# A graph network's second edge scatter on GpSimd: issued in portions beside the first layer's attention, router and experts, instead of all beside the experts

## What is computed

```python
edge_index = jnp.stack([src, dst])
xn = _layernorm(x, axis=-1)
x = x + _L0_gnn_ref(xn, edge_index, ...) + _L0_mix_ref(xn[None], L0_mix_Wq, L0_mix_Wkv, L0_mix_Wproj, L0_mix_bproj)[0]
x = x + _L0_ffn_ref(_layernorm(x, axis=-1)[None], ...)[0]      # router and 6 experts, top 2
xn = _layernorm(x, axis=-1)
x = x + _L1_gnn_ref(xn, src, dst, ...) + _L1_mix_ref(xn[None], ...)[0]
...
```

## Time and profile before

| | |
|---|---|
| median of three executions | 7550.93 us (7548.48 to 7556.42) |
| profiled execution, its own time | 7552.14 us |
| its span in the profile | 7550.2 us |
| granted TensorE clock, mean | 0.838 of full speed |
| busy: TensorE matmuls | 5770.7 us, 76% |
| busy: VectorE / ScalarE / GpSimd | 4088.7 / 2739.3 / 3202.7 us |

### The profile page before, as it was taken

The page is one execution under the profiler, slowest core; times in us unless marked ns, Lnnn a source line. Parts: engine busy times, 40 slices in busy tenths (PEclk is TensorE's granted clock), DMA queues, the critical chain, the costliest instruction groups (busy, mean ns, idle before and its releaser), DMA issues. The chain is left out here.

```text
span 7550.2 us, 91454 instructions
## 1 busy us (share of the span) xinstructions
PE 5770.7 (76%) x22573; PEld 3591.7 (48%) x22664; DVE 4088.7 (54%) x9995; ACT 2739.3 (36%) x7575; POOL 3202.7 (42%) x3209
## 2 busy tenths in 40 slices
PE   5564688888985788876976787998788858998386
PEld 3332355554542565642545553554455535565253
DVE  7876577733113899966245334213577775556401
ACT  2524477721220444410114432113166615555010
POOL 1776576404772666610017750000177715553101
PEclk9999788888997778778988887898778766987597
DMA  2534222100001655510013330000144423333222
GB/s 87 165 86 155 50 50 47 31 12 28 2 2 53 172 158 157 159 32 13 0 60 105 105 75 23 0 0 14 47 117 115 112 58 105 98 98 69 76 99 74
DMA packets 268803, 549.15 MB, mean 73 GB/s; under 512 B 86992, under 2 KB 136588, under 8 KB 263692
## 3 DMA queue, kind: packets, MB, share of 16 engines
q0 software_dynamic: 134496, 314.63, 16.6%
q1 hardware_dynamic: 133932, 230.20, 9.5%
HBM read 495.56 MB, written 49.00 MB: 72 GB/s over the span
## 5 line engine op out<-in xcount | busy, mean ns | idle before, releaser
L1252 POOL DMA_INDIRECT L_edges_rows<-scratch_L_kv,L_edges_index x416 | 496.8, 1194 | 379.7 <-PE L_edges_ps_sum L1501 213.0
L1252 POOL DMA_INDIRECT L3a_edges_rows<-scratch_L3a,L3a_edges_index x416 | 462.5, 1112 | 409.5 <-DMA L3a_edges_last<-order_dst_last 257.1
L1252 POOL DMA_INDIRECT L3b_edges_rows<-scratch_L3b,L3b_edges_index x416 | 398.6, 958 | 400.8 <-PE L3b_edges_ps_sum L1501 236.3
L1702 POOL TENSOR_TENSOR L_norm_fold<-L_norm_square 128x400 f32<-128x400 f32 x64 | 66.6, 1040 | 1168.3 <-ACT L_norm_square L1711 1168.3
L482 POOL DMA_INDIRECT scratch_by_dst<-dst_record,dst_dest x400 | 439.7, 1099 | 271.1 <-DVE dst_dest L334 149.5
L1252 POOL DMA_INDIRECT L_edges_rows<-scratch_L,L_edges_index x416 | 424.4, 1020 | 257.3 <-issue 117.8
L632 POOL DMA_INDIRECT L_edges_rows<-scratch_L,L_edges_index x416 | 396.8, 954 | 274.5 <-SPq L616 148.0
L2324 DVE TENSOR_TENSOR L_experts_gated_h<-L_experts_hidden,L_experts_ps_g 128x800 f32<-128x800 f32 x112 | 110.6, 988 | 665.0 <-PE L_experts_ps_g L2277 665.0
L482 POOL DMA_INDIRECT scratch_by_src<-src_record,src_dest x400 | 383.1, 958 | 124.0 <-issue 121.7
L2315 ACT ACTIVATE L_experts_hidden<-L_experts_ps_h,L_eb_sb 128x400 f32<-128x400 f32 x320 | 190.2, 594 | 646.2 <-PE L_experts_ps_h L2270 646.2
L1373 DVE TENSOR_TENSOR L_acc<-L_edges_ps_sum,L_acc 128x264 f32 (+1 forms) x832 | 357.0, 429 | 98.5 <-DVE L_acc L1373 70.2
(11 more groups left out here) (767 smaller groups left out, 13541.3 us busy)
## 6 DMA issues: line engine op xcount, KB each, us to landing
x<-scratch_dst_key_rows SPq DMA_DIRECT2D x50, 512.0 KB, 4.7
x<-scratch_src_key_rows SPq DMA_DIRECT2D x50, 512.0 KB
L_experts_w<-in_L_w SPq DMA_DIRECT2D x16, 1024.0 KB
L_edges_rows<-scratch_L,L_edges_index POOLq DMA_INDIRECT x832
L_edges_lo_rows<-order_src_lo_rows SPq DMA_DIRECT2D x52, 256.0 KB
L3a_edges_lo_rows<-order_dst_lo_rows SPq DMA_DIRECT2D x52, 256.0 KB
L3b_edges_lo_rows<-order_dst_lo_rows SPq DMA_DIRECT2D x52, 256.0 KB
x<-scratch_dst_lo_rows SPq DMA_DIRECT2D x50, 256.0 KB, 3.7
```

Source lines behind the costliest of these rows:

```text
L1252: pool.indirect_dma_start(rows[:, n % RING, k, 0:RW], None, row_table, bass.IndirectOffsetOnAxis(index[:, t:t + 1].bitcast(U32), 0)).then_ ...
```

## The change

The 400 scatters of the order by `src` go through a new class `Scatter`, which keeps how many are done. `some(pool, count)` issues the next `count` scatters (waiting, as before, at the start of each round of 8 for the round four before it). `layers`, `context` and `attention_out` get a GpSimd function that, for each chunk or tile, waits for a matmul result and then calls `beside(pool)`; `experts` calls it once per step, after the step's gate matmul. A new stage `landed` after layer 0 issues what is left and waits for all landings; `close` then clears the four semaphores, with one more barrier.

```diff
+class Scatter:
+    def __init__(self, nc, order):
+        self.nc, self.order, self.done = nc, order, 0
+        self.landed = [nc.alloc_semaphore(f"later_scattered{b}") for b in range(4)]
+
+    def some(self, pool, count):
+        for t in range(self.done, min(self.done + count, ET)):
+            n = t // SB
+            if t % SB == 0 and n >= 4:
+                pool.wait_ge(self.landed[n % 4], n // 4 * (16 * SB))
+            pool.indirect_dma_start(self.order["table"], bass.IndirectOffsetOnAxis(self.order["dest"][:, t:t + 1], 0),
+                                    self.order["record"][:, t, :], None).then_inc(self.landed[n % 4], 16)
+            self.done = t + 1
+
+    def rest(self, pool):
+        self.some(pool, ET)
+        for b in range(4):
+            pool.wait_ge(self.landed[b], len(range(b, ET // SB, 4)) * (16 * SB))
+
+    def close(self):
+        self.nc.clear_and_free_semaphores(self.landed)
+        self.nc.all_engine_barrier()
...
 (layers)
+            @block.gpsimd
+            def _(pool):
+                if beside:
+                    for c in range(NC):
+                        if acts:
+                            pool.wait_ge(made_act, c * acts + 1)
+                        else:
+                            pool.wait_ge(made_dve, c * dves + 1)
+                        beside(pool)
...
 (context)
+            @block.gpsimd
+            def _(pool):
+                if beside:
+                    for t in range(NT):
+                        pool.wait_ge(made, t + 3)
+                        beside(pool)
...
 (experts)
-                if to_scatter:
-                    scatter_slots(pool, to_scatter, scattered)
+                if beside:
+                    for n in range(STEPS):
+                        pool.wait_ge(gate_made, n + 1)
+                        beside(pool)
...
 (attention_out)
+            @block.gpsimd
+            def _(pool):
+                if beside:
+                    for c in range(NC):
+                        pool.wait_ge(passed, 2 * c + 1)
+                        beside(pool)
...
 (layer0)
-        linear_attention(kit, "L0_mix", m, xn, wq, wk, wv, wp, spread, x, 1e-6, 0.0, 1.0, bias=bp)
+        linear_attention(kit, "L0_mix", m, xn, wq, wk, wv, wp, spread, x, 1e-6, 0.0, 1.0, bias=bp,
+                         besides=(lambda pool: later.some(pool, 3), lambda pool: later.some(pool, 2),
+                                  lambda pool: later.some(pool, 6)))
...
-            layers(kit, "L0_router", [Layer(r1, xn, rh, bias=rb1, func="relu")])
+            layers(kit, "L0_router", [Layer(r1, xn, rh, bias=rb1, func="relu")], beside=lambda pool: later.some(pool, 2))
...
-        experts(kit, "L0_experts", xn, x, [e1, e2, e3], [eb1, eb2], eb3, comb_t, ACT.Relu, to_scatter=later)
+        experts(kit, "L0_experts", xn, x, [e1, e2, e3], [eb1, eb2], eb3, comb_t, ACT.Relu, beside=lambda pool: later.some(pool, 6))
...
+def landed(kit, later):
+    with Stage(kit, "later_rest"):
+        with kit.nc.Block() as block:
+            @block.gpsimd
+            def _(pool):
+                later.rest(pool)
+    later.close()
...
 (program)
+            later = Scatter(nc, later)
             layer0(kit, x, xn, to_dst, scratch, later)
+            landed(kit, later)
```

More of the change, by code:

```diff
@@ L1772, in bank_free, with layers @@
     return j + 1 if j >= 4 else j + 4 * ((n - 1 - j) // 4) + 5 - n
-def layers(kit, name, stack, loads=(), last=None):
+def layers(kit, name, stack, loads=(), last=None, beside=None):
     nc = kit.nc
@@ L2023, in _, with context @@
                     dve.wait_ge(taken, t + 1)
-def context(kit, name, ksrc, wk, vsrc, wv, halves, out, elu, den=None, col_scale=None, scale=1.0):
+def context(kit, name, ksrc, wk, vsrc, wv, halves, out, elu, den=None, col_scale=None, scale=1.0, beside=None):
     nc = kit.nc
@@ L2226, in _, with experts @@
                 link(v.tensor_tensor(comb[:, :, 0:E_], one[0][:], one[1][:], ALU.add))
-def experts(kit, name, xnt, x, weights, biases, last_bias, comb_t, func, to_scatter=None):
+def experts(kit, name, xnt, x, weights, biases, last_bias, comb_t, func, beside=None):
     nc = kit.nc
@@ L2244, in experts @@
             s.sem(n) for n in ("made", "taken", "gate_made", "gated", "result", "added"))
-        scattered = [s.sem(f"scattered{b}") for b in range(4)]
         def chunk(n):
@@ L2616, in _, with linear_attention, attention_out @@
                     dve.wait_ge(out_done, c + 2)
-def linear_attention(kit, name, m, xn, wq, wk, wv, wo, spread, dst, floor, plus, shrink, bias=None):
+def linear_attention(kit, name, m, xn, wq, wk, wv, wo, spread, dst, floor, plus, shrink, bias=None, besides=(None, None, None)):
     q = m(f"{name}_q", [P, 2, NP])
     ctx, den = m(f"{name}_ctx", [P, 2, D]), m(f"{name}_den", [P, 2, DEN + HEADS * NC])
-    layers(kit, f"{name}_queries", [Layer(wq, xn, q, func="elu1")])
-    context(kit, f"{name}_context", xn, wk, xn, wv, 2, ctx, True, den=den, scale=1.0 / shrink)
-    attention_out(kit, f"{name}_out", q, ctx, den, spread, wo, dst, floor, plus, shrink, bias)
+    layers(kit, f"{name}_queries", [Layer(wq, xn, q, func="elu1")], beside=besides[0])
+    context(kit, f"{name}_context", xn, wk, xn, wv, 2, ctx, True, den=den, scale=1.0 / shrink, beside=besides[1])
+    attention_out(kit, f"{name}_out", q, ctx, den, spread, wo, dst, floor, plus, shrink, bias, besides[2])
 HEADS = 8
 DEN = HEADS * (NC - 1)
-def attention_out(kit, name, q, ctx, den, spread, wo, dst, floor, plus, shrink, bias=None):
+def attention_out(kit, name, q, ctx, den, spread, wo, dst, floor, plus, shrink, bias=None, beside=None):
     nc = kit.nc
```

## The result

Six runs of each kernel on one chip: before 7549.70 us (7536.44 to 7556.42), after 7508.83 us (7494.19 to 7513.03). The ratio is 0.9944, with a 95% interval from 0.9931 to 0.9957: 41 us faster by the medians. The two profiled executions, 7552.14 and 7502.26 us, lie 49.9 us apart.

What follows compares the result with a forecast made beforehand. GpSimd's 400 scatters, 1.263 us each, were taken to outlast the experts, leaving 81.3 us of GpSimd alone. 79.0 - 19.1 (overhang and barriers) - 9.1 (drains) - 2 (clock) = 48.8 us gained, hence 7502 us, range 7490 to 7534.

Steps and rivals of the forecast that it cites:

- The gain, 79.0 us: Experts' end: GpSimd's lone tail goes, so `prepare_src` starts at 2240.2 instead of 2319.2.
- What hangs over, 17.6 us in queries, context and out: Scatters outlasting their stages, drains excluded: 1.0 us in queries, 6.5 in context, 10.1 in out.
- The drains, 9.1 us: GpSimd's drains at four block exits: 2.1, 2.6, 2.5 and 1.9 us in queries, context, out and router.
- The clock, 2 us in norm2: Norm2's beginning: a lower TensorE clock after some 13 us without matmuls costs 2 us, bounds 0 and 7.
- Nothing for contention: Four attention and router stages: a scatter beside VectorE work keeps its 958 ns, costing nothing extra.
- Nothing for the pacing: All stages with scatters: GpSimd's waits on matmuls cost nothing, as no one waits for it inside a stage.
- Rival 2: Attention: contention makes scatters 1.40 us each or copies hold GpSimd up; gain 32 to 38 us, chance 0.08.
- Rival 1: Block exits: every drain behind scatters costs 9.2 us whatever their number; gain 18 us, 7533 us, chance 0.13.
- Rival 3: Block exits behind unlanded scatters: drains of 16.7 us make the kernel slower, 7570 us, chance 0.04.
- Rival 4: Experts: GpSimd reaches portions late and the tail stays; gain 20 to 45 us, some 7515 us, chance 0.03.

Runs made afterwards that it cites:

- the last kernel: The change with portions of 2, 1, 4 and 2 in queries, context, out and router, and 7, 7, 6 in turn in the experts: 7478.34 us, ratio 0.9911.
- The drain kernel: The change plus 12 small stages behind layer 0 with none to 400 scatters, with or without landing waits or idle time: 9805.45 us, only drains used.
- the duel: The change plus eight small stages, one engine alone or two in turns, most beside scatters: TensorE-ScalarE turn 2.29 us on first kind, up to 5.60 on second.
- either mix: The change with 2, 1, 5, 2 and 7, 6, 6 in turn in the experts (7494.43 us, ratio 0.9925), or the last kernel.

## Why the prediction was right

The forecast was 7502 us, in a range from 7490 to 7534; 7508.83 was measured, and the profiled run gives 7502.26 for the 7503.3 of the sum. The mechanism held: the stages are as long as their slowest engine, and GpSimd's issuing and its drains set what the move gains and costs. Two terms were off and nearly cancel.

- *The gain, 79.0 us.* The experts and the landed stage take 438.05 us from entry to `prepare_src`'s first DMA, before 516.71: 78.7. The last portion ends 36 us ahead of VectorE (38 said), the hand-over takes 2.33 us (2.3 said).
- *What hangs over, 17.6 us in queries, context and out.* They grew by 3.6, 10.8 and 14.3 us, 28.7 together; less their drains (2.2 + 4.1 + 4.0) that is 18.4. Portions that fit (34.0, 63.5, 65.4 us in the last kernel) take nearly all of the 28.7 back with scatters still beside these stages, which shows that it is what hangs over, scatters and drain, and nothing else.
- *The drains, 9.1 us.* This is the mis-sized term: they took 2.2 + 4.1 + 4.0 + 1.8 = 12.1. I had drawn a line from 25 DMAs to 400, 19 ns each. The drain kernel shows 82 ns each, and that 400 is no point of that line: somewhere above 96 the growth ends. 24, 50, 48 and 16 by the measured line are 2.0, 4.1, 4.0 and 1.4. The assumption beside it, that a drain is bound to the count and not to how long ago the last DMA was, holds. For the experts I said 6.6 and it was 5.93.
- *The clock, 2 us in norm2.* Norm2 grew by 0.6. But I had no term for the router and what follows. The router became 0.9 us shorter, where 3.4 more were booked: its portion and drain did hang over by 3.3, but its clock was 0.90 for 0.71, and its matmuls took 14.27 us instead of 18.54. The last kernel confirms it: the same 16 scatters at a clock of 0.72 make 30.8 us. The logit rows gave 2.0 back at 0.50, which is 1.2 GHz throughout, for 0.61; ahead of them TensorE had been idle for 5.06 us, before for 1.72. Against the sum, the clock thus gave 1.4 + 4.2 - 2.0 = 3.6 us, and drains and overhang took 3.0 + 0.8 = 3.8. That they cancel is luck.
- *Nothing for contention.* 962 ns for 958, and DVE's busy time in the context is 21.59 for 21.37. Rival 2 is out. The Trainium skill, "SBUF — State Buffer", section "Who interferes with whom", says that a VectorE instruction with at most one SBUF input, outside the 2-port modes, doesn't contend with GpSimd. The trace agrees: beside the context's 25 copies, which read PSUM, GpSimd was busy 48.02 us with 50 scatters, 960 ns each.
- *Nothing for the pacing.* On the first kind of chip no run speaks against it: the experts' 48 steps average 8.93 us with 400 unpaced scatters beside them and with paced ones alike. On the second kind the kernel before takes 72.8 us a step beside its unpaced scatters, and the pacing is worth 308 us (744.0 - 436.0), more than all my terms together. The forecast was right for the first kind alone, and nothing in it says so; that the runs it was held against were of that kind was not its doing.

Rival 1 (each drain 9.2 us) is out, though 9.2 and more does occur beyond 96 scatters. Rival 3 had a true core: records of 15 and 19 us appear in the change too. But what exceeds 4 us in them is scatters still being made, as its "against" said. Rival 4 fell with the 36 us of margin.

From the queries' first matmul to `prepare_src`'s first DMA the difference is -48.2 us, of 49.9 between the profiled runs. The medians lie 40.9 apart; the profiled run of before is 2.4 us above its median and that of after 6.6 below. These 9 us were not traced to a stage. By the medians alone, the gain is 41 us where 49 were forecast.

**What stays open.** Why engines start late on the second kind of chip, and whether it is the chip at all. What the raster of 0.70 us is, why the turns of ScalarE and VectorE escape it, and why it sets in sooner in the experts than in the duel. Where the drain's growth ends between 96 and 192 scatters, and what orders it beyond. No run shows either mix on the second kind; by its portions of 7, the faster one of them may lose some of its lead there.

## What to carry to other kernels

Work that an idle engine does inside other stages is free only while each portion fits its step: sum up (first result + n periods) against the stage's end, and take the portion one smaller where it overruns; here this, with more of the scatters in the experts, was worth another 25 us by the ratios. A block that ends behind indirect DMAs pays GpSimd's drain, some 82 ns for each of up to 96 of them. Waiting doesn't shorten it; it is hidden only where another engine ends later still. And leave gaps in long runs of indirect DMAs: here it cost nothing on one kind of chip, and on the other the experts took 308 us less with it, 3.6% of the kernel.

## What was not expected of the hardware

- One kernel, two kinds of chip: 7540 to 7550 us and 8728 to 8776 us, and 1195 of the 1200 us between two profiles in stages with long runs of indirect DMAs. The ratio of the same change is 0.9944 on one and 0.952 on the other.
- There, after 36 to 45 us of indirect DMAs without a gap, TensorE's turns with ScalarE or VectorE go from 2.3 to 5.60 us, ScalarE and VectorE alone from 0.6 to 1.40 us, at a DMA share of 0.03. In the experts it sets in within 20.5 us. Pauses of 1.4 us on average behind every 6 scatters were enough to prevent it there, 0.1 us behind every 7 were not.
- GpSimd's drain: 50 ns + 82 ns for each indirect DMA up to 96; 2.0 to 14.0 us beyond, with no order in the count (286 scatters 7.89, 311 scatters 2.01; 400 scatters 5.28, 9.20 and, in the kernel before on the second kind, 13.97).
